# One transformer layer on one core: a group later for the softmax normalisation, four banks for the last tiles, one chain of statistics

## The chip, the cores and the metric

The kernel runs on one core of a Trainium2 chip. The metric is the device time of one execution in microseconds (us). The profiler's page and trace come from one further execution, whose own time is given beside them.

## The reference

What is computed, cut to its core (4 batches of 1024 tokens of 256 numbers, 16 heads of 64, 32 experts with 1024 hidden numbers, all in float32):

```python
xn = (x - mean(x)) / sqrt(var(x) + 1e-5)
# attention, causal, q and k turned by the rotary table
q, k, v = heads(xn @ Wq), heads(xn @ Wk), heads(xn @ Wv)
attn = softmax(causal(rope(q) @ rope(k).T * 64 ** -0.5)) @ v
# experts choose tokens: the 8 likeliest tokens of each expert, over the softmax along the tokens
probs = softmax(xn @ gate_w.T + gate_b, axis=tokens)
vals, idx = top_k(probs, 8)
merged = sum_k(vals * xn[idx])                       # one row per batch and expert
h = gelu([merged, 1] @ w1[e]);  o = [h, 1] @ w2[e]
moe = zeros_like(x).at[idx].add(vals * o)
out = x + attn @ Wo + bo + moe
```

## The kernel before, in words

A pair is two heads of one batch. There are 8 pairs to a batch (`PAIRS`) and 32 in all (`N`). The program of every engine is one loop over `STAGES`, the list of (P, g) with pair P and group g = 0..5, after two groups of pair -1 that stand in for a beginning, and with pair 32 as a tail that has no scores. Within a stage each engine issues its instructions in an order written out by hand. Groups later or earlier in the list are reached by an index, as in `STAGES[s - 3]`.

In one group TensorE (PE) makes the scores of two chunks of the current pair into the PSUM tiles pA and pB (L1388 to L1400), makes the scores of the next pair once more for their row maxima, into bank 0 of pC and into pA (L1412, L1419), makes one projection into pF (the "fill": L1465 for q and k, L1448 for v), may do one further piece of work (below), multiplies the exponentials with V into pO (L1490), and twice per pair sums the exponentials' partial sums into pC (L1499).

The other engines follow it. VectorE (DVE) takes the maxima (L1065), which PE awaits before it goes on to the further piece of work; it combines them (L1072), makes the shift t_D from them (L1079), and does the rotary steps (L1099, L1089). ScalarE (ACT) takes the exponentials into t_PT (L812), evicts the projections (t_raw, L834) and rounds them (t_HI, L844). GpSimd (POOL) adds up the exponentials (t_acc, L732, L735), does two rotary steps (L710, L713) and adds the bias to the input rows (t_xb, L745). SyncE (SP) issues most DMAs in one queue of instructions: the swap of neighbouring rows for the rotary step (t_swap, L623), loads and stores.

**Normalising.** A half pair n (64 of them) ends in this chain: PE sums (L1499), ACT evicts (L861), SP stores the row (s_s, L522) and loads it spread over partitions (t_comp, L527), DVE inverts it (`invert`, L1049), SP stores it (r_s, L532) and loads it broadcast into the place t_OT (L553), and DVE multiplies the attention's output into it (`normalise`, L1057). `invert` runs two stages after the half pair's sums, `normalise` three stages after, as the last DVE instruction of its stage. For batch 0 SP then stores the normalised rows (o0_s, L658), to be loaded back when the output tiles of this batch are made.

**The further pieces.** Pairs 5 to 13 have the experts' work, in 4-expert groups, as slots: layer 1 (PE L1514, L1519), a turn, and layer 2; DVE reads each slot's bank. Output tiles of 128 tokens are 16 or 24 matmuls with Wo and one matmul with the spread matrix t_wsp of the experts: those of batch 0 in pairs 14 and 15 (L1546, L1548, rows t_os loaded by SP L682), of batches 1 and 2 in pairs 16, 17 and 24, 25 (L1540), from t_oh (rounded by ACT, L879) and t_ol (the rest, DVE L1133). The last batch's tiles are made in two pieces: `part` over seven pairs (L1561, L1564) in pairs 31 and 32, kept by DVE (`keep`, L1157), and `last` for pair 31 (L1573) at the end, finished by DVE (`finish`, L1163). ACT L887 and DVE L1150 round for the parts, in two buffers. The banks of these tiles are bank 1 of pC and of pB in turn (`out_bank`).

**Statistics.** The layer norm of batches 1 to 3 is prepared in pairs 0 to 2: bn_stats (L1171) and a chain of seven small dependent DVE instructions per batch (L1176 to L1184), a root on ACT (L893), and six more small ones (L1191 and on, `moments`). Units (L1595, L1624) transpose the rows of x, and are spread over pairs 1 to 3.

## Time and profile before

| what | value |
|---|---|
| time, median of 3 runs | 1408.34 us (1407.0 to 1410.91) |
| the profiled execution's own time | 1406.38 us |
| its span | 1404.6 us, mean granted TensorE clock 0.986 |
| PE, busy | 1331.6 us, 95% of the span |
| POOL, busy | 970.3 us, 69% |
| DVE, busy | 878.1 us, 63% |
| ACT, busy | 635.2 us, 45% |
| DMA read and written | 130.71 MB and 22.54 MB |

"L1057" is line 1057 of the kernel. A busy share says how much of the span an engine worked; which of them sets the end is to be read from the waits. The granted clock is that of TensorE, as a share of its 2.4 GHz.

### The profile page before, as it was taken

What the parts mean: (1) busy time and instruction counts of PE and PEld (TensorE: products, weight loads), DVE (VectorE), ACT (ScalarE), POOL (GpSimd) and SP (SyncE); (2) the same over time, 40 slices, a digit from 0 to 9 for tenths busy, and PEclk for the clock granted to TensorE, in tenths of its full rate; (3) what the DMA queues carried; (4) which work ended last, traced back from release to release, by engine and by line L of the source; (5) the groups of instructions that cost most, each with busy time, mean ns of one, the idle gap of its engine ahead of it and who ended that gap; (6) DMA issues with size and microseconds to landing.
All of it is one profiled execution on the core that took longest, in us unless ns stands there. A gap on an engine that the chain in (4) does not pass through costs nothing.

```text
span 1404.6 us, 31395 instructions
## 1 busy us (share of the span) xinstructions
PE 1331.6 (95%) x11612; PEld 867.7 (62%) x11612; DVE 878.1 (63%) x1202; ACT 635.2 (45%) x963; POOL 970.3 (69%) x661
## 2 busy tenths in 40 slices
PE   6889999999999999999999999999999999999987
PEld 5556566555655555546676776666656776666655
DVE  5797767666565556556347666666666566666633
ACT  3446565453445334524224434444444344554431
POOL 2666688765566656656566777888778668888842
PEclk9999999999999999999999999999999999999999
DMA  5324333669667866665642222212232221212121
GB/s 177 122 84 145 114 134 116 226 211 320 213 230 244 287 215 221 212 235 171 180 137 81 66 75 65 77 62 77 96 102 91 74 76 55 84 62 77 47 58 57
DMA packets 122752, 188.86 MB, mean 134 GB/s; under 512 B 29616, under 2 KB 57808, under 8 KB 122608
## 3 DMA queue, kind: packets, MB, share of 16 engines
q1 hardware_dynamic: 92176, 112.51, 24.4%
q10 hardware_dynamic: 30384, 74.23, 15.4%
q8 instruction: 100, 1.64, 0.5%
q14 instruction: 44, 0.36, 0.1%
q0 software_dynamic: 48, 0.13, 0.1%
HBM read 130.71 MB, written 22.54 MB: 109 GB/s over the span
## 4 chain that ended last, share of the span: by engine, by line
PE 79%; DMA 7%; DVE 5%; issue 4%; ACT 4%; SPq 1%; POOL 0%; ACTq 0%; DVEq 0%; POOLq 0%
PE t_pO L1490 17%; PE t_pF L1465 11%; PE t_pA L1388 9%; PE t_pB L1388 6%; PE t_pF L1448 6%; DMA t_swap<-t_raw 3%; PE t_pA L1412 3%; PE t_pC L1412 3%; PE t_pA L1393 2%; PE t_pC L1499 2%; PE t_pB L1393 2%; PE t_pB L1540 2%; PE t_pC L1540 2%; PE t_pB L1514 1%; ACT t_PT L812 1%
## 5 line engine op out<-in xcount | busy, mean ns | idle before, releaser
L735 POOL TENSOR_TENSOR t_acc<-t_acc,t_PT 128x1024 f32<-128x1024 f32 (+3 forms) x256 | 437.9, 1711 | 161.8 <-ACT t_PT L812 141.6
L710 POOL TENSOR_TENSOR t_swap<-t_swap,t_sin 128x512 f32<-128x512 f32 x124 | 163.8, 1321 | 198.9 <-DMA t_swap<-t_raw 198.3
L1490 PE MATMUL t_pO<-t_PT,t_V 128*64 128x512 f32 (+3 forms) x1536 | 294.1, 504 | 4.7 <-issue 4.7
L812 ACT ACTIVATE t_PT<-t_pA 128x1024 f32<-128x1024 f32 x192 | 169.7, 884 | 273.1 <-PE t_pA L1400 234.7
L1465 PE MATMUL t_pF<-t_xT,t_wqk 128*128 128x512 f32 x756 | 211.2, 415 | 5.3 <-issue 3.0
L1490 PEld LDWEIGHTS t_pO<-t_PT,t_V 128*64 128x64 f32 x1536 | 94.3, 137 | 145.7 <-issue 129.3
L713 POOL TENSOR_TENSOR t_rot<-t_rot,t_swap 128x512 f32<-128x512 f32 x124 | 174.1, 1404 | 10.8 <-DVE t_rot L1099 1.2
L1465 PEld LDWEIGHTS t_pF<-t_xT,t_wqk 128*128 128x128 f32 x756 | 133.9, 190 | 41.3 <-issue 13.8
L834 ACT ACTIVATE t_raw<-t_pF 128x512 f32<-128x512 f32 x124 | 74.0, 597 | 180.5 <-PE t_pF L1465 136.6
L1089 DVE TENSOR_TENSOR t_LO<-t_rot,t_HI 128x512 fp32r<-128x512 f32 x124 | 147.1, 1186 | 7.5 <-ACT t_HI L844 7.5
L732 POOL TENSOR_TENSOR t_acc<-t_PT 128x768 f32<-128x768 f32 x64 | 142.9, 2232 | 9.6 <-ACT t_PT L812 9.6
L1065 DVE TENSOR_REDUCE t_nm<-t_pC 128x2 f32<-128x256 f32 (+2 forms) x96 | 71.8, 777 | 122.0 <-PE t_pC L1419 121.6
L812 ACT ACTIVATE t_PT<-t_pB 128x768 f32<-128x768 f32 (+1 forms) x192 | 141.9, 739 | 2.9 <-PE t_pB L1393 2.1
L1057 DVE TENSOR_TENSOR t_OT<-t_OT,t_OC 128x512 f32<-128x512 f32 x64 | 83.5, 1305 | 56.1 <-DMA t_OT<-r_s 56.1
L1065 DVE TENSOR_REDUCE t_nma<-t_pC 128x2 f32<-128x1024 f32 x66 | 80.7, 1222 | 54.2 <-PE t_pC L1412 54.1
L1448 PE MATMUL t_pF<-t_wvs,t_xT 128*128 128x256 f32 x756 | 106.6, 290 | 2.2 <-issue 2.1
L1448 PEld LDWEIGHTS t_pF<-t_wvs,t_xT 128*128 128x128 f32 x756 | 94.0, 190 | 11.8 <-issue 10.4
L1099 DVE TENSOR_TENSOR t_rot<-t_pF,t_cos 128x512 f32<-128x512 f32 x124 | 85.0, 685 | 22.4 <-ACT t_raw L834 19.1
L861 ACT ACTIVATE t_srow<-t_pC 128x256 f32<-128x256 f32 x64 | 24.6, 385 | 161.1 <-PE t_pC L1499 161.0
L1079 DVE TENSOR_TENSOR t_D<-t_pB,t_sel 128x512 fp32r<-128x512 f32 x64 | 43.9, 686 | 79.1 <-PE t_pB L1476 79.1
L1388 PE MATMUL t_pA<-t_HI 64*128 64x512 f32 (+1 forms) x384 | 88.9, 460 | 4.2 <-DVE t_nma L1065 2.7
L1388 PEld LDWEIGHTS t_pA<-t_HI 64*128 64x128 f32 x384 | 35.8, 183 | 85.1 <-issue 78.0
(228 smaller groups left out, 2465.3 us busy)
## 6 DMA issues: line engine op xcount, KB each, us to landing
t_w1t<-in_L_ffn_w ACTq DMA_DIRECT2D x32, 1024.0 KB, 5.5
t_w2t<-in_L_ffn_w ACTq DMA_DIRECT2D x32, 1024.0 KB, 8.4
t_swap<-t_raw SPq DMA_DIRECT2D x248, 128.0 KB, 2.1
t_OT<-r_s SPq DMA_DIRECT2D x128, 128.0 KB, 2.9
...
```

The source lines that it names most:

```text
L710: pool.tensor_tensor(swap_of(r), swap_of(r), sin[:, c * BANK:(c + 1) * BANK], ALU.mult).then_inc(sin_sem, 1)
L713: pool.tensor_tensor(rot_of(r), rot_of(r), swap_of(r), ALU.add).then_inc(rot_sem, 1)
L732: pool.tensor_tensor(a[:, :, off:], first[:, :, off:], pt, ALU.add).then_inc(acc_done, 1)
L735: pool.tensor_tensor(a[:, :, off:], a[:, :, off:], pt, ALU.add).then_inc(acc_done, 1)
L812: act.activation(PT[:, n % PTS, :, 0:w], bank[:, :, 0:w], ACT.Exp, scale=SCALE).then_inc(exp_done, 1)
L1065: op = dve.tensor_reduce(dst, bank[:, :, at:at + w], AX_X, ALU.max, negate=True)
L1089: dve.tensor_tensor(LO[:, P % 2, z, q], rot_of(r), HI[:, P % 2, z, q].bitcast(F32), ALU.subtract).then_inc(lo_done, 1)
L1099: dve.tensor_tensor(rot_of(r), fill_bank(f), cos[:, c * BANK:(c + 1) * BANK], ALU.mult).then_inc(cos_done, 1)
L1388: pe.matmul(bank[:, h, 0:w], hk[d, P % 2, 1, k], hq[d, P % 2, 0, q], start=(a == 0), stop=False)
L1448: mm = pe.matmul(bank[:, u * 2 * P128:(u + 1) * 2 * P128], xT[:, c, hx, k, q], wvs[:, hw, k, :], start=(a == 0), stop=(a == 3 * KT - 1))
L1465: mm = pe.matmul(bank, wqk[:, hw, k, z * P128:(z + 1) * P128], xT[:, c, hx, k, :], start=(a == 0), stop=(a == 3 * KT - 1))
L1490: mm = pe.matmul(pO[h * DH:(h + 1) * DH, off:], v, PT[:, n % PTS, h, 0:w], start=(j == 0), stop=(j == 4 * c + 3))
```

## The change

Four edits are made at once.

1. `normalise` on DVE moves from the end of the third stage after the sums into the middle of the fourth (after the maxima, the shift, the rotary steps and `invert`, ahead of the reads of slots and tiles). The last three of the 64 half pairs stay at the third stage. SP's store of the normalised rows of batch 0 goes one stage later too.
2. The output tiles of batch 0 are made one group later, (14,2) to (15,3) in place of (14,1) to (15,2), and their loads are issued one stage later; the first of them loses its special place behind the values.
3. The last batch's parts are rounded in three buffers instead of two, at stages of a list of their own (`ROUND_AT`); their banks are bank 1 of pC and pF, and they stand ahead of the wait for the second chunk's exponentials. Its last matmuls use four banks.
4. The statistics of batches 1 to 3 are one chain over all 24 tiles at (1,1), one root on ACT and one `moments` at (1,2), in place of three of each; batch 1's normalisation and its units move one group later.

The third buffer, oh3 and ol3, takes the place of xT, so a rounding into it waits until the last fill is done.

```diff
--- before.py
+++ after.py
@@ -113,7 +113,7 @@
 
     y, p = divmod(P, PAIRS)
     if MOE + E // GE <= P <= MOE + E // GE + 1:
-        n = (P - MOE - E // GE) * GROUPS + g - 1
+        n = (P - MOE - E // GE) * GROUPS + g - 2
         return [(0, n)] if 0 <= n < NT else []
     if P == N:
         tiles = {2: (0, 1, 2, 3), 3: (4, 5, 6, 7)}.get(g, ())
...
@@ -125,20 +125,22 @@
 PARTS_AT = {(N - 1, 1): [0], (N - 1, 2): [1], (N - 1, 3): [2], (N - 1, 4): [3], (N - 1, 5): [4], (N, 1): [5], (N, 2): [6, 7]}
 
 
+ROUND_AT = {(N - 1, 0): [0], (N - 1, 1): [1], (N - 1, 2): [2, 3], (N - 1, 3): [4], (N - 1, 4): [5], (N - 1, 5): [6], (N, 0): [7]}
+
+
 def parts_of(P, g):
 
     return PARTS_AT.get((P, g), [])
 
 
-UNITS_AT = {(0, 5): ("logit", 0), (1, 3): ("x", 1, 0), (1, 4): ("x", 1, 1), (2, 2): ("logit", 1), (2, 3): ("x", 2, 0),
+UNITS_AT = {(0, 5): ("logit", 0), (1, 4): ("x", 1, 0), (1, 5): ("x", 1, 1), (2, 2): ("logit", 1), (2, 3): ("x", 2, 0),
             (2, 4): ("x", 2, 1), (3, 2): ("logit", 2), (3, 3): ("x", 3, 0), (3, 4): ("x", 3, 1), (4, 2): ("logit", 3),
             (5, 0): ("gates",), (5, 1): ("merge",), (5, 2): ("merged",)}
 UNIT = {u: n for n, u in enumerate(UNITS_AT.values())}
 DOUBLE = {u: n for n, u in enumerate([u for u in UNIT if u[0] in ("x", "logit", "gates")])}
 UNIT_STEP = {u: UNIT[u] + sum(DOUBLE[v] < len(DOUBLE) and UNIT[v] < UNIT[u] for v in DOUBLE) for u in UNIT}
-STATISTICS_AT = {(0, 2): [(1, 0)], (0, 3): [(1, 1)], (0, 4): [(2, 0)], (0, 5): [(2, 1), (3, 0)], (1, 0): [(3, 1)]}
-MOMENTS_AT = {(1, 1): 1, (1, 4): 2, (2, 1): 3}
-NORM_AT = {(1, 2): (1, 0), (1, 3): (1, 1), (2, 2): (2, 0), (2, 3): (2, 1), (3, 2): (3, 0), (3, 3): (3, 1)}
+STATISTICS_AT = {(0, 2): [(1, 0)], (0, 3): [(1, 1)], (0, 4): [(2, 0)], (0, 5): [(2, 1)], (1, 0): [(3, 0)], (1, 1): [(3, 1)]}
+NORM_AT = {(1, 3): (1, 0), (1, 4): (1, 1), (2, 2): (2, 0), (2, 3): (2, 1), (3, 2): (3, 0), (3, 3): (3, 1)}
 NORM = {h: n for n, h in enumerate([(0, 0), (0, 1)] + list(NORM_AT.values()))}
 
 
...
@@ -257,7 +259,8 @@
         mT = sb("t_mT", [P128, GE, KT, 32])
         hT = sb("t_hT", [P128, 2, P128])
         with nc.sbuf_tensor("t_yp", [P128, NT, C], F32) as yp, nc.sbuf_tensor("t_wlast", [P128, C], F32) as wlast:
-            pass
+            with nc.sbuf_tensor("t_oh3", [P128, PAIRS - 1, P128], F32R) as oh3, nc.sbuf_tensor("t_ol3", [P128, PAIRS - 1, P128], F32R) as ol3:
+                pass
         xT = sb("t_xT", [P128, 2, 2, KT, BANK], F32R)
         wqk = sb("t_wqk", [P128, 2, KT, 2 * P128], F32R)
         wvs = sb("t_wvs", [P128, 2, KT, 2 * P128], F32R)
...
@@ -418,14 +421,28 @@
         y_stored = [sem(f"t_y_stored{i}") for i in range(2)]
         block = ctx.enter_context(nc.Block())
 
+        def rows_of(n):
+            return (slice(1, B), slice(0, NT)) if n == 2 else (0, slice(4 * n, 4 * n + 4))
+
         def next_outputs(s):
             return outputs_of(*STAGES[s + 1]) if s + 1 < len(STAGES) else []
 
-        def next_parts(s):
-            return parts_of(*STAGES[s + 1]) if s + 1 < len(STAGES) else []
+        def normalised_at(s):
+            late = normalise_of(*STAGES[s - 4]) if s >= 4 else None
+            soon = normalise_of(*STAGES[s - 3]) if s >= 3 else None
+            return [n for n in (late,) if n is not None and n < 2 * N - 3] + [n for n in (soon,) if n is not None and n >= 2 * N - 3]
 
         def parts_before(s):
             return sum(len(parts_of(*t)) for t in STAGES[:s])
+
+        def part_buffers(t):
+            return (oh3[:, :, :], ol3[:, :, :]) if t % 3 == 2 else (oh[:, t % 3, 0:PAIRS - 1, :], ol[:, t % 3, 0:PAIRS - 1, :])
+
+        def part_bank(t):
+            return (pC[:, 1, 0:C], pF[:, 0:C])[t % 2]
+
+        def last_bank(t):
+            return (pC[:, 1, 0:C], pF[:, 0:C], pB[:, 1, 0:C], pA[:, 1, 0:C])[t % 4]
 
         def fill_bank(f):
...
@@ -513,7 +530,7 @@
                             load_b2(G + 1)
 
             def tiles_ahead(P, g):
-                n = (P - MOE - E // GE) * GROUPS + g
+                n = (P - MOE - E // GE) * GROUPS + g - 1
                 return [0, 1] if n == -1 else [n + 2] if 0 <= n < NT - 2 else []
 
             def store_sums(n):
...
@@ -652,7 +669,7 @@
                     start_output(P // PAIRS)
                 if (P, g) == (N - 2, 5):
                     start_output(B - 1)
-                n = normalise_of(*STAGES[s - 4]) if s >= 4 else None
...
@@ -881,20 +898,22 @@
             def round_part(t):
 
                 act.wait_ge(o_done, 2 * (N - 2) + t // 4 + 1)
-                act.wait_ge(y_mm, (B - 1) * NT - 1 + min(t, 1))
-                if t >= 2:
-                    act.wait_ge(y_part, t - 1)
-                act.activation(oh[:, t % 2, 0:PAIRS - 1, :], OT[:, 0:PAIRS - 1, t * P128:(t + 1) * P128], ACT.Copy).then_inc(oh_done, 1)
+                act.wait_ge(y_mm, (B - 1) * NT)
+                if t == 2:
+                    act.wait_ge(proj_done, len(FILL))
+                if t >= 3:
+                    act.wait_ge(y_part, t - 2)
+                act.activation(part_buffers(t)[0], OT[:, 0:PAIRS - 1, t * P128:(t + 1) * P128], ACT.Copy).then_inc(oh_done, 1)
...
@@ -1023,9 +1042,8 @@
                     weights_high(w)
                 if (P, g) in UNITS_AT:
                     unit(UNITS_AT[P, g])
-                if (P, g) == (1, 1):
-                    for n in range(2, B + 1):
-                        root(n)
+                if (P, g) == (1, 2):
+                    root(2)
                 if (P, g) in NORM_AT:
...
@@ -1038,7 +1056,7 @@
                 for y, t in next_outputs(s):
                     if y in (1, 2):
                         round_out(y, t)
-                for t in next_parts(s):
+                for t in ROUND_AT.get((P, g), []):
                     round_part(t)
 
         @block.vector
...
@@ -1144,34 +1162,37 @@
             def rest_of_part(t):
 
                 dve.wait_ge(oh_done, (B - 2) * NT + t + 1)
-                dve.wait_ge(y_mm, (B - 1) * NT - 1 + min(t, 1))
-                if t >= 2:
-                    dve.wait_ge(y_part, t - 1)
-                dve.tensor_tensor(ol[:, t % 2, 0:PAIRS - 1, :], OT[:, 0:PAIRS - 1, t * P128:(t + 1) * P128],
-                                  oh[:, t % 2, 0:PAIRS - 1, :].bitcast(F32), ALU.subtract).then_inc(ol_done, 1)
+                dve.wait_ge(y_mm, (B - 1) * NT)
+                if t == 2:
+                    dve.wait_ge(proj_done, len(FILL))
+                if t >= 3:
+                    dve.wait_ge(y_part, t - 2)
+                high, low_part = part_buffers(t)
+                dve.tensor_tensor(low_part, OT[:, 0:PAIRS - 1, t * P128:(t + 1) * P128],
+                                  high.bitcast(F32), ALU.subtract).then_inc(ol_done, 1)
 
             def keep(t):
 
                 dve.wait_ge(y_part, t + 1)
                 dve.wait_ge(xb_done, (B - 1) * NT + t + 1)
-                dve.tensor_tensor(yp[:, t, :], out_bank(t), xb[:, t % 2, :], ALU.add).then_inc(y_kept, 1)
+                dve.tensor_tensor(yp[:, t, :], part_bank(t), xb[:, t % 2, :], ALU.add).then_inc(y_kept, 1)
 
             def finish(t):
 
                 dve.wait_ge(y_mm, (B - 1) * NT + t + 1)
                 dve.wait_ge(y_kept, NT)
-                dve.tensor_tensor(yp[:, t, :], out_bank(t), yp[:, t, :], ALU.add).then_inc(y_done, 1)
-
-            def statistics(n, h):
-
-                b = n - 1 if n > 1 else 0
-                c = slice(0, NT) if n > 1 else slice(4 * h, 4 * h + 4)
-                done = stat_done[n]
+                dve.tensor_tensor(yp[:, t, :], last_bank(t), yp[:, t, :], ALU.add).then_inc(y_done, 1)
+
+            def spread(b, h):
+
                 for t in range(4 * h, 4 * h + 4):
                     st = dve.bn_stats(stats[:, b, t, :], xn[:, b, t, :])
-                if n > 1 and h == 0:
-                    return
-                st.then_inc(done, 1)
+                return st
+
+            def statistics(n):
...
@@ -1322,8 +1345,7 @@
                 n = normalise_of(*STAGES[s - 2]) if s >= 2 else None
                 if n is not None:
                     invert(n)
-                n = normalise_of(*STAGES[s - 3]) if s >= 3 else None
-                if n is not None and P == N:
+                for n in normalised_at(s):
                     normalise(n)
                 w = weights_of(P, g)
...
@@ -1332,12 +1354,15 @@
                     unit(UNITS_AT[P, g])
                 for b, h in STATISTICS_AT.get((P, g), []):
                     dve.wait_ge(xb_loaded[b - 1], 32)
-                    statistics(b + 1, h)
+                    st = spread(b, h)
+                    if (b, h) == (B - 1, 1):
+                        st.then_inc(stat_done[2], 1)
+                        statistics(2)
                 if (P, g) == (0, 2):
                     dve.wait_ge(g_hi, 1)
                     dve.tensor_tensor(gThl[:, 1, :, :, :], gT[:, :, :, :], gThl[:, 0, :, :, :].bitcast(F32), ALU.subtract).then_inc(g_lo, 1)
-                if (P, g) in MOMENTS_AT:
-                    moments(MOMENTS_AT[P, g] + 1)
+                if (P, g) == (1, 2):
+                    moments(2)
...
                         rest(y, t)
-                for t in next_parts(s):
+                for t in ROUND_AT.get((P, g), []):
                     rest_of_part(t)
-                n = normalise_of(*STAGES[s - 3]) if s >= 3 else None
-                if n is not None and P < N:
-                    normalise(n)
 
...
@@ -1549,16 +1571,20 @@
 
             def part(t):
 
-                bank = out_bank(t)
+                bank = part_bank(t)
                 if t >= 2:
                     pe.wait_ge(y_kept, t - 1)
                 else:
                     pe.wait_ge(y_done, (B - 1) * NT)
+                    pe.wait_ge(max_done, MAXES[N, 0])
+                    pe.wait_ge(fill_read, len(VFILL))
+                    pe.wait_ge(cos_done, len(ROPE))
                 pe.wait_ge(ol_done, (B - 2) * NT + t + 1)
+                high, low_part = part_buffers(t)
                 a = 0
...
@@ -1566,11 +1592,12 @@
             def last(t):
 
                 pe.wait_ge(y_kept, NT)
-                if t >= 2:
-                    pe.wait_ge(y_done, (B - 1) * NT + t - 1)
+                pe.wait_ge(exp_done, N * len(CHUNKS))
+                if t >= 4:
+                    pe.wait_ge(y_done, (B - 1) * NT + t - 3)
                 pe.wait_ge(wo_loaded, 32)
                 pe.wait_ge(o_done, 2 * (N - 1) + t // 4 + 1)
-                pe.matmul(out_bank(t), OT[:, PAIRS - 1, t * P128:(t + 1) * P128], wlast[:, :],
+                pe.matmul(last_bank(t), OT[:, PAIRS - 1, t * P128:(t + 1) * P128], wlast[:, :],
                           start=True, stop=True).then_inc(y_mm, 1)
...
@@ -1690,6 +1716,8 @@
                     maximum(pair, MAXES[P, g] + m, (pC, pA)[m % 2], pieces)
                 if fill_of(P, g) and not after_gelu:
                     fill(fill_of(P, g))
+                for t in parts_of(P, g):
+                    part(t)
                 if chunks:
                     pe.wait_ge(exp_done, chunk_index(*chunks[1]) + 1)
                 if g == 1 and 0 <= P < N:
@@ -1703,20 +1731,16 @@
                 for x_ in slots:
                     if x_[0] == "turn":
                         slot(*x_)
-                for t in parts_of(P, g):
-                    part(t)
                 for y, t in outputs_of(P, g):
                     if y == B - 1:
                         last(t)
-                    elif not first_tile:
+                    else:
                         output(y, t)
                 for x_ in slots:
                     if x_[0] == "layer1":
                         slot(*x_)
                 for chunk in chunks:
                     values(*chunk)
-                if first_tile:
-                    output(0, 0)
                 for x_ in slots:
                     if x_[0] == "layer2":
                         slot(*x_)
```

## Rows read from the trace of the kernel before

**Rows 1.** The page's first part: busy time and share by engine.
```profile
PE 1331.6 (95%) x11612; PEld 867.7 (62%) x11612; DVE 878.1 (63%) x1202; ACT 635.2 (45%) x963; POOL 970.3 (69%) x661
```

**Rows 2.** Whom PE waited for: us in total, times, longest.
```profile
PE t_pB L1514 <- issue: 17.4, 8, 3.3
...
PE t_pO L1490 <- issue: 4.7, 3, 2.3
...
PE t_pC L1595 <- issue: 2.8, 1, 2.8
PE t_pA L1388 <- DVE t_nma L1065: 2.7, 1, 2.7
...
PE t_pB L1514 <- DVE t_nmb L1065: 1.7, 1, 1.7
...
PE t_pA L1393 <- DVE t_D L1079: 1.1, 1, 1.1
```

**Rows 3.** Timeline around one slot: start, us, engine line op, idle before.
```profile
387.30 0.69 DVE L1057 TENSOR_TENSOR t_OT<-t_OT,t_OC 128x512 f32<-128x512 f32 x1 [3.89 <-DMA t_OT<-r_s]
387.91 1.22 DVE L1065 TENSOR_REDUCE t_nma<-t_pC 128x2 f32<-128x1024 f32 x1
...
388.91 0.60 ACT L834 ACTIVATE t_raw<-t_pF 128x512 f32<-128x512 f32 x1 [2.27 <-DMA t_swap<-t_raw]
...
389.22 1.07 PE L1514 MATMUL t_pB<-t_w1t,t_mT 128*32 128x256 f32 x16 [1.83 <-issue]
```

**Rows 4.** Windows: length, busy PE, PEld, DVE, ACT, POOL, granted clock, DMA share, GB/s.
```profile
1350.00:1395.00 45.00, 37.52 (x297) 27.82 (x293) 11.97 (x19) 13.56 (x18) 19.00 (x14) 1.00 0.12 36
1395.00:1402.00 7.00, 4.44 (x17) 2.55 (x16) 4.42 (x10) 0.00 (x0) 0.00 (x0) 1.00 0.27 93
72.00:86.00 14.00, 11.28 (x93) 7.72 (x90) 13.03 (x23) 3.63 (x6) 10.70 (x7) 0.88 0.06 21
338.00:348.00 10.00, 7.10 (x61) 3.20 (x59) 7.93 (x11) 1.68 (x4) 4.99 (x4) 0.83 0.96 338
619.00:632.00 13.00, 9.66 (x68) 4.49 (x66) 4.92 (x7) 2.96 (x5) 8.99 (x7) 0.74 0.49 162
```

**Rows 5.** The chain of waits that ended last, stretch 380 to 392 us.
```profile
by line: DMA t_swap<-t_raw 99.2%; SPq L623 7.9%; SPq L553 5.1%; ACT t_raw L834 5.0%; SPq L658 4.9%; issue 2.5%; SPq L621 0.1%; ACTq L468 0.1%
```

**Rows 6.** Line L1057: idle time of DVE before it.
```profile
  DMA t_OT<-r_s: 56.1, 23
```

**Rows 7.** Timeline of batch 0's first two output tiles, PE and SP.
```profile
672.84 3.72 PE L1546 MATMUL t_pC<-t_wo,t_os 128*128 128x256 f32 x16
...
677.52 0.43 SPq L682 DMA_DIRECT2D t_os<-o_s  x1
...
678.44 0.70 PE L1548 MATMUL t_pC<-t_oe,t_wsp 128*128 128x256 f32 x2 [1.88 <-DMA t_oe<-o_s]
...
685.08 2.11 PE L1546 MATMUL t_pB<-t_wo,t_os 128*128 128x256 f32 x9
```

**Rows 8.** Line L682: the loads of batch 0's tiles.
```profile
DMA to landing us min/median/max: 4.3/4.9/5.5
```

**Rows 9.** Timeline where batch 1's first output tile begins.
```profile
772.97 2.33 DVE L1133 TENSOR_TENSOR t_ol<-t_OT,t_oh 128x1024 fp32r<-128x1024 f32 x1
...
775.69 0.48 PE L1540 MATMUL t_pC<-t_woh,t_oh 128*128 128x256 f32 x2
```

**Rows 10.** DVE timeline of the statistics chains: two of the three.
```profile
73.10 0.93 DVE L1176 TENSOR_TENSOR t_both<-t_stats 128x8 f32<-128x8 f32 x1
...
76.75 1.76 DVE L1184 SCALAR_TENSOR_TENSOR t_ve<-t_gap,t_mse 128x8 f32<-128x8 f32 x1
...
88.35 0.17 DVE L1176 TENSOR_TENSOR t_both<-t_stats 128x8 f32<-128x8 f32 x1
...
89.07 0.17 DVE L1184 SCALAR_TENSOR_TENSOR t_ve<-t_gap,t_mse 128x8 f32<-128x8 f32 x1
```

**Rows 11.** POOL timeline of the last pair.
```profile
1366.57 0.73 POOL L745 TENSOR_TENSOR t_xb<-t_xin,t_bob 128x256 f32<-128x256 f32 x1
```

24 lines of the change are left out of this document (14 added, 10 removed).

## The prediction

> **What bounds the kernel now.** I read the page's busy shares first. PE works for 1331.6 us, 95% of its span, and the next engine, POOL, for 69% [rows 1]. So time can only come out of PE: out of the 73.0 us in which it stands still (1404.6 less 1331.6), and out of stretches in which its clock was lowered. I then read whom PE waited for [rows 2], went to the timeline at each of the longer waits, to see which instruction was late [rows 3], and last to windows around them, for the granted clock [rows 4].
>
> The waits before L1514, the first matmul of a layer-1 slot, are the largest group: 17.4 us in 8 waits, put down to "issue", and 1.7 us in one more [rows 2]. The timeline shows what they are. DVE stood 3.9 us before `normalise`, until the broadcast load t_OT<-r_s had landed; it then worked 0.7 us, and only then came to the next stage's first maxima (387.91, 1.22 us). PE, which must see those maxima before it goes on to the slot, started it at 389.22, 0.1 us after they ended [rows 3]. So `normalise` as the last DVE instruction of a stage passes a DMA's lateness to PE. After the longest such gaps the clock is low: 0.83 of 2.4 GHz over the 10 us from 338, and 0.74 over the 13 us from 619 [rows 4]. Two more stretches of 10 us, from 572 and from 1038, are like the first, so there are three of these and one of the other.
>
> **a. `normalise` a group later: -26.8.** The multiplication comes after the maxima, the shift and the rotary steps of the stage behind, some 7 us (1404.6 us over 198 stages is 7.1) after its present place. The load that it waits for has then landed, since the longest wait seen is about 4 us. What goes is 17.4 + 1.7 before the slots, and before the values (L1490) the longest wait of 2.3 and 1.0 of the other 2.4 [rows 2], which begin the same way: 22.4. The clock comes back with it. The mean of 0.83 over 10 us loses 1.7 us if PE had work all the while, and 0.17 of its 7.10 busy us, 1.2, if it counts for those alone; 0.74 over 13 us loses 3.4 or 2.5 [rows 4]. Three of the first and one of the second are 8.5 or 6.1; I take 7.4, near the middle. Against this, in the same stretch ACT's eviction t_raw waited 2.27 us for the swap's DMA and began at 388.91 [rows 3], with only 0.3 us between it and PE's start. When DVE no longer delays PE, that DMA does a little later: PE's next fill needs the bank. I put this at 0.4 in each of 8 steps, 3. The sum is -22.4 - 7.4 + 3 = -26.8. The bounds are -10 (the swap takes most of it back) and -31 (nothing eroded, the clock wholly back). The price of the move itself is nothing in busy time: the same 64 instructions. They stand ahead of the slot reads now, so what is queued behind a late load is no longer the maxima but a slot's read; that is rival D.
>
> **b. Rounding where a batch ends: +3.2.** The first tiles of batches 1 and 2 need the pair before them normalised. Now the rest t_ol is worked out at 772.97 to 775.30 and PE uses it at 775.69 [rows 9]. With `normalise` about one rotary step, one shift and one low part later, ACT's rounding and the rest come some 2 us later, of which 0.4 is slack: 1.6, twice. Bounds 0 (it hides) and +4.
>
> **c. Batch 0's tiles: +3.0.** PE waited 1.88 us in the first tile for t_oe, until 678.44 [rows 7]; that goes. But the tile loads are now issued behind SP's instructions that start the output, at the place of the one at 677.52 [rows 7], and land 4.3 to 5.5 us later, median 4.9 [rows 8]: 682.4. Without the tile at 672.84 PE starts the next group then and comes to its tile after what it now does between 679.14 (678.44 + 0.70) and 685.08, 5.9 us, of which I take off 0.8 for the lowered clock seen there: 678.0. It waits 4.4, 2.5 more than now, and I add 0.5 for the clock after a longer gap. Bounds 0 (the group before hides it) and +6.
>
> The Trainium skill ("DMA: Bandwidth & Descriptors", section "Issuing engines are not separate DMA queues") says that DMAs of all issuing engines run on the same 16 DMA engines and interleave. By that rule the two tile loads issued together would share with each other and with the swap; if this doubled the 4.9 us of [rows 8], c would be +7.9 in place of +3.0. No row of before has two tile loads at once under load.
>
> **d. The early block: -3.9.** PE waited 2.7 us for the maxima t_nma and 1.1 for t_D, each behind a statistics chain on DVE, and 2.8 before a unit (L1595) behind the third `moments` [rows 2]; the clock was 0.88 over the 14 us from 72, which is 1.7 [rows 4]. Together 8.3, all gone with the chains. The one chain is no longer than one of the three in instructions, but lands at (1,1). Its price depends on POOL: from 73.10 to the end of 76.75 + 1.76 the seven took 5.4 us while POOL was adding up exponentials, from 88.35 to 89.24 0.9 us while it stood still [rows 10]. At (1,1) POOL is adding up. I take the middle, 3, as what reaches PE (2.9), and 1.5 for the clock: -8.3 + 4.4 = -3.9. Bounds -8 (0.9, hidden) and +2 (a chain of 5.4 in full, the waits for `moments` at (1,2) behind the root, and the lowered clock).
>
> The Trainium skill ("GPSIMD Engine Reference", section "1. Specifications") lists that GpSimd's SBUF interfaces are shared with VectorE, with contention for DVE instructions in a 2-port mode or with two SBUF inputs. This speaks against the merged chain at its new place; the 5.4 against 0.9 us of [rows 10] agree. By it the upper price would hold, 2.4 more than I take, and d would be -1.5.
>
> **e. The tail: -7.3.** Between 1350 and 1395 PE is busy for 37.52 of 45 us, so 7.5 us are idle: about half before parts that wait for exponentials, half before the two last parts, which wait for their rounding in two buffers; from 1395 to 1402 it is busy for 4.44 of 7 [rows 4]. Parts placed ahead of the wait for exponentials fill the first half, a third buffer takes the second. The four banks of the last tiles bring 0.7 of the 2.6 us in the last stretch. But t_xb comes from POOL behind two accumulations, as at 1366.57 [rows 11], and with it y_kept, for which part t+2 waits: +0.9. The sum is -7.5 - 0.7 + 0.9 = -7.3. Bounds -4 and -9.
>
> **Sum.** -26.8 + 3.2 + 3.0 - 3.9 - 7.3 = -31.8. From the profiled execution's own 1406.38 (span 1404.6 and 1.8 around it) this makes 1374.6. The median of the runs is 1408.34, 2.0 above the profiled one, so I forecast 1376.5.
>
> **Rivals.**
> B: The swap's DMA takes DVE's place. In the stretch of [rows 5] the chain that ends last is 99.2% the DMA t_swap<-t_raw, with ACT's t_raw behind it [rows 3]. For it: DMA share 0.96 in the window from 338 [rows 4]. Against it: the share is 0.49 in the window from 619, where the clock was lowest [rows 4], and the fill's bank is needed only a stage later. Half of a, 13.4, is then lost: 1390. Chance 0.15.
> C: The tail is set by POOL. Then parts wait for y_kept instead of exponentials, 3.7 of e go, and 0.8 more for bias sums: 1381. For it: two accumulations of the exponentials precede each bias sum, as at 1366.57 [rows 11]. Against it: the sum for part t is wanted only two parts later. Chance 0.09.
> D: The change doesn't do what it says: the load is late in the new place too, or DVE's reads of the slot banks behind it stop PE the same. Then a is 0: 1403.4, at the edge of no change. Against it: a whole group between. Chance 0.07.
> E, slower: `normalise` in the middle is where DVE has no slack, and all of DVE's 56.1 us of standing before it (23 waits) [rows 6] fall on PE, not 22.4 as now. Then a is not -26.8 but +33.7: 1376.5 + 60.5 = 1437. It decides once the waits in the new place cost PE 32 us more than I forecast. Against it: the load is given a group more. Chance 0.05.
>
> **How the numbers follow.** My forecast has 0.64; its own range is 1368 to 1386, from the bounds of a to e taken partly together. Range for 8 in 10: 1364, where a, d and e come near their lower ends, to 1394, which takes in B and C; D and E, and the far ends of a, lie outside. 0.3% is 4.2 us, about what a measurement here tells from no change, so faster means below 1404.1. Forecast, B and C are faster, and half of D: 0.91. The other half of D is the same: 0.04. E is slower: 0.05.
>
> **What would show it.** The profile after should have PE's waits before L1514 and its successor lines under 4 us in all, a granted clock near 1.0 in the windows where it was 0.83 and 0.74, and nearly no idle time of DVE before `normalise`. Right for c: a wait of PE in batch 0's first tile for t_os of about 4 us. Right for d: one chain of 3 us or more at (1,1), with a wait of PE in (1,2) behind it. Right for e: no wait for t_PT before the parts and none for t_ol. The forecast is wrong if PE's idle time stays above 50 us, or if new waits on ACT's t_raw, on t_swap or on y_kept stand where the old ones did.

## The result, and the profile after

The changed kernel takes 1393.24 us (median, 1389.95 to 1395.02) against 1409.21 us for the kernel before, measured beside it: ratio 0.9885, 95% interval 0.9861 to 0.9909, so 16 us faster. Measured once more, further below, it was 0.9871 (0.983 to 0.9911). The forecast was a fall of 31.8 us; it came to half.

The profiled execution took 1393.71 us, 12.7 less than the profiled one of before. The first parts of the page of the changed kernel:

```profile
span 1391.9 us, 31373 instructions
...
PE 1330.1 (96%) x11612; PEld 870.8 (63%) x11612; DVE 855.6 (61%) x1176; ACT 634.5 (46%) x961; POOL 975.7 (70%) x661
```

PE is as busy as before (1331.6 in [rows 1]), so nearly all of the gain is idle time: 61.8 us are left of 73.0. Whom PE waited for in the changed kernel (us in total, times, longest):

```profile
PE t_pF L1470 <- DMA t_wvs<-wv_s: 9.1, 3, 3.6
...
PE t_pC L1568 <- DMA t_os<-o_s: 4.9, 1, 4.9
PE t_pO L1512 <- issue: 4.4, 1, 4.4
...
PE t_pB L1410 <- ACT t_PT L829: 3.0, 3, 1.0
PE t_pF L1470 <- issue: 2.8, 4, 0.9
...
PE t_pB L1410 <- DVE t_g L1133: 2.3, 4, 1.0
```

The waits before the layer-1 slots, 17.4 and 1.7 us in [rows 2], are gone, and so are those before the values at 1038.67 and 1172.41. The one before the values now listed is in pair 1. New are 9.1 us in three waits for the load of t_wvs, 4.9 us for t_os, and eight of 0.3 to 1.0 us before L1410, the scores of a stage's second chunk. DVE has no idle time left before `normalise` (L1075 after; 56.1 us in [rows 6]).

Windows of the changed kernel (length, busy PE, PEld, DVE, ACT, POOL, clock, DMA share, GB/s):

```profile
340.00:350.00 10.00, 9.40 (x89) 5.38 (x87) 5.95 (x12) 5.33 (x9) 5.57 (x6) 1.00 1.06 367
350.00:360.00 10.00, 6.38 (x50) 5.22 (x48) 2.97 (x5) 6.64 (x9) 7.24 (x7) 0.76 0.64 239
535.00:550.00 15.00, 11.94 (x90) 7.60 (x90) 5.93 (x9) 6.43 (x11) 9.34 (x7) 0.77 0.30 110
1034.00:1044.00 10.00, 9.54 (x88) 5.75 (x87) 6.20 (x8) 6.14 (x11) 9.36 (x8) 1.00 0.41 134
1337.00:1382.00 45.00, 43.33 (x356) 32.55 (x357) 16.08 (x25) 16.42 (x23) 23.77 (x19) 1.00 0.16 41
1382.00:1389.00 7.00, 5.00 (x24) 3.51 (x22) 4.24 (x10) 0.00 (x0) 0.00 (x0) 1.00 0.31 103
```

The stretch near 1038 has its clock back (0.83 before), and so have those from 572 and from 619, where the granted clock is now 1.00. The one from 350 has not: 0.76, behind a wait of 3.6 us. In the tail PE is busy for 43.33 of 45 us (37.52 in [rows 4]).

To see where the 12.7 us went, I set the start of one and the same score matmul (L1388 before, L1410 after, counted from the first) in the two traces side by side. This is a table made from the two timelines:

```
before    after   after less before   stretch that ends here                       change
  58.31    62.17   +3.9               the start; no edit touches it                 +3.9
 260.16   266.01   +5.9               pairs 1 to 4                                  +2.0
 632.94   627.75   -5.2               pairs 5 to 13, the experts                   -11.0
 649.33   644.42   -4.9                                                             +0.3
 755.21   754.63   -0.6               batch 0's output tiles                        +4.3
1033.54  1033.50    0.0               first tiles of batch 1, pairs up to 23        +0.5
1048.59  1044.51   -4.1               the wait at 1038.67                           -4.0
1167.85  1164.18   -3.7               first tiles of batch 2                        +0.4
1179.40  1174.72   -4.7               the wait at 1172.41                           -1.0
1316.02  1311.33   -4.7               to pair 31                                     0.0
1404.6   1391.9   -12.7               the tail, to the end of the span              -8.0
```

The +3.9 of the start is in a part that no edit touches. In the traces of the further runs below the same mark lies between 58.5 and 64.3 us, so it is a difference between executions, and of the size of what separates -12.7 from -16.

### The profile page after: what moved, and what is told of

It reads as the page before. It is cut to its first block, busy times and chain, and to the rows that moved or that the text cites. A ratio compares the mean times of both kernels' runs of the same rounds, so it can differ in the third digit from the quotient of the medians.

```text
span 1391.9 us, 31373 instructions
## 1 busy us (share of the span) xinstructions
PE 1330.1 (96%) x11612; PEld 870.8 (63%) x11612; DVE 855.6 (61%) x1176; ACT 634.5 (46%) x961; POOL 975.7 (70%) x661
## 4 chain that ended last, share of the span: by engine, by line
PE 79%; DMA 8%; DVE 5%; issue 3%; ACT 2%; SPq 1%; POOL 1%; ACTq 0%; DVEq 0%; POOLq 0%
PE t_pO L1512 17%; PE t_pF L1487 11%; PE t_pA L1410 9%; PE t_pF L1470 7%; PE t_pB L1410 7%; DMA t_swap<-t_raw 4%; PE t_pA L1434 3%; PE t_pC L1434 3%; PE t_pA L1415 2%; PE t_pC L1521 2%; PE t_pB L1415 2%; PE t_pC L1562 2%; PE t_pB L1562 2%; DMA t_wvs<-wv_s 1%; PE t_pC L1568 1%
## 5 line engine op out<-in xcount | busy, mean ns | idle before, releaser
L727 POOL TENSOR_TENSOR t_swap<-t_swap,t_sin 128x512 f32<-128x512 f32 x124 | 167.8, 1353 | 183.7 <-DMA t_swap<-t_raw 183.2
L730 POOL TENSOR_TENSOR t_rot<-t_rot,t_swap 128x512 f32<-128x512 f32 x124 | 180.4, 1455 | 9.7
L1107 DVE TENSOR_TENSOR t_LO<-t_rot,t_HI 128x512 fp32r<-128x512 f32 x124 | 142.5, 1149 | 7.4 <-ACT t_HI L861 7.4
L749 POOL TENSOR_TENSOR t_acc<-t_PT 128x768 f32<-128x768 f32 x64 | 140.1, 2189 | 8.3 <-ACT t_PT L829 8.3
L1410 PE MATMUL t_pA<-t_HI 64*128 64x512 f32 (+1 forms) x384 | 89.1, 460 | 2.5 <-DVE t_nmb L1083 2.5
L1410 PEld LDWEIGHTS t_pA<-t_HI 64*128 64x128 f32 x384 | 35.8, 183 | 82.9 <-issue 78.3
L1083 DVE TENSOR_REDUCE t_nmb<-t_pC 128x2 f32<-128x256 f32 (+1 forms) x62 | 31.7, 554 | 87.3 <-PE t_pC L1441 87.3
L1434 PE MATMUL t_pC<-t_HI 64*128 64x512 f32 (+2 forms) x448 | 78.9, 372 | 4.2 <-ACT t_HI L861 2.1
```

The costliest lines, as they stand in the source:

```text
L727: pool.tensor_tensor(swap_of(r), swap_of(r), sin[:, c * BANK:(c + 1) * BANK], ALU.mult).then_inc(sin_sem, 1)
L730: pool.tensor_tensor(rot_of(r), rot_of(r), swap_of(r), ALU.add).then_inc(rot_sem, 1)
L749: pool.tensor_tensor(a[:, :, off:], first[:, :, off:], pt, ALU.add).then_inc(acc_done, 1)
L1083: op = dve.tensor_reduce(dst, bank[:, :, at:at + w], AX_X, ALU.max, negate=True)
L1107: dve.tensor_tensor(LO[:, P % 2, z, q], rot_of(r), HI[:, P % 2, z, q].bitcast(F32), ALU.subtract).then_inc(lo_done, 1)
L1410: pe.matmul(bank[:, h, 0:w], hk[d, P % 2, 1, k], hq[d, P % 2, 0, q], start=(a == 0), stop=False)
```

## The experiments

All ratios are against the kernel before, measured beside the kernels in question. There are three such groups (e1 to e4, e5 to e8, e9 to e11), each on a chip of its own; the kernel before had medians of 1413.46, 1413.66 and 1412.89 us in them, and its runs spread over 1400 to 1426 us. An interval is 4 to 8 us to each side.

**Edit 1 alone.** The kernel before with:

```diff
-                n = normalise_of(*STAGES[s - 3]) if s >= 3 else None
-                if n is not None and P == N:
+                for n in normalised_at(s):
                     normalise(n)
...
-                n = normalise_of(*STAGES[s - 3]) if s >= 3 else None
-                if n is not None and P < N:
-                    normalise(n)
```

and the store of batch 0 at `s - 5`.

> The kernel before with edit 1 alone (normalise in the middle of the fourth stage, the store of batch 0 one stage later). Theory X, a load that is late next: the waits before the layer-1 slots and before the values (22.4 us) go, but PE then waits for the load t_wvs<-wv_s, which SP issues behind the swap and the stores of a slot: about 9 us in three waits and 3 us of lowered clock, as in the changed kernel. Net of the pairs with experts -11, of the later pairs -5, and 3 to 5 us lost in pairs 1 to 5 where normalise now stands ahead of the reads of the units' banks: 10 to 14 us below the kernel before. Theory Y, my forecast as it stood: the t_wvs wait in the changed kernel comes from something else among its edits, and edit 1 alone gives -27. Theory Z: edit 1 gives nothing or little, and the changed kernel's gain comes from its tail.

Measured: 1405.15 us, ratio 0.9938 (0.9905 to 0.997), 8.8 us faster. Whom PE waited for:

```profile
PE t_pF L1449 <- DMA t_wvs<-wv_s: 9.9, 3, 3.4
...
PE t_pB L1389 <- ACT t_PT L817: 3.0, 3, 1.0
...
PE t_pB L1389 <- DVE t_g L1120: 2.3, 3, 1.5
```

The waits before the slots are gone and 9.9 us of waits for t_wvs have come, with edits 2, 3 and 4 absent. They belong to edit 1. My forecast as it stood (-27) falls; theory X's count of waits holds, its sum is a little too good (-10 to -14, against an interval of -4 to -13). It had put the loss in pairs 1 to 5 at 3 to 5 us; the trace has pairs 1 to 4 alone 7.4 us longer than the trace of before (the table at the end of this section).

**The load two groups earlier.** The changed kernel with:

```diff
-                unit = (P + 1) // 2
-                if g == 0 and P % 2 and PAIRS // 2 <= unit < N // 2:
+                unit = P // 2 + 1
+                if g == 4 and P >= 0 and P % 2 == 0 and PAIRS // 2 <= unit < N // 2:
```

> The changed kernel with one more edit: SP issues the load of t_wvs for pair P+1 at group 4 of pair P (P even), two groups ahead of its place before. Theory X, the load is only issued late: its three waits of 3.6, 3.1 and 2.4 us go and the clock of these stretches comes back, 10 to 12 us below the changed kernel, so some 26 to 28 below the kernel before. Theory V, the pairs with experts are held by the transfers of w1 and w2 whatever the order: the waits only move to another load (t_w1t, t_w2t, t_swap), and no more than 3 us go.

Measured: 1397.77 us, ratio 0.9872 (0.9813 to 0.9932), the same as the changed kernel (0.9871 and 0.9885). Waits and, under it, the timeline at one of them:

```profile
PE t_pB L1410 <- DVE t_g L1133: 10.0, 5, 2.8
```

```profile
348.58 0.60 ACT L851 ACTIVATE t_raw<-t_pF 128x512 f32<-128x512 f32 x1 [4.56 <-DMA t_swap<-t_raw]
...
349.21 0.69 DVE L1117 TENSOR_TENSOR t_rot<-t_pF,t_cos 128x512 f32<-128x512 f32 x1 [3.55 <-ACT t_raw L851]
...
349.82 0.68 DVE L1075 TENSOR_TENSOR t_OT<-t_OT,t_OC 128x512 f32<-128x512 f32 x1
...
350.42 0.42 DVE L1133 TENSOR_TENSOR t_g<-t_pB,t_b 128x256 f32<-128x256 f32 x1
...
350.89 0.33 PE L1410 MATMUL t_pB<-t_HI 64*128 64x128 f32 x2 [2.23 <-DVE t_g L1133]
```

The waits for t_wvs went, and 10.0 us in 5 waits stand before L1410 instead. The load itself, issued earlier, took 5.2 us at the median and up to 9.0, against 3.6 and 7.1 in the changed kernel. The timeline reads backwards: PE starts once DVE has read the slot's bank (350.42), which stood behind `normalise` (349.82) and the rotary step (349.21), which waited for ACT's t_raw (348.58), which had waited 4.56 us for the swap's DMA. Theory X, that the load was only issued late, falls. This is my rival B's chain, but it appears only once the other transfer is out of its way.

**Edit 4 undone.** The changed kernel with the three chains, roots and moments of the kernel before.

```diff
-                    if (b, h) == (B - 1, 1):
-                        st.then_inc(stat_done[2], 1)
-                        statistics(2)
+                    if h == 1:
+                        st.then_inc(stat_done[b + 1], 1)
+                        statistics(b + 1)
```

> The changed kernel with edit 4 undone: three statistics chains, roots and moments as in the kernel before. Theory S, the merged chain costs more than the three: the wait of 4.4 us before the values at 104.9 and its lowered clock (about 2) go, but the wait of 2.7 at 78 with its clock (4.5 together), the one of 1.1 at 101 and the one of 2.8 at 143 come back: within 3 us of the changed kernel. Theory F, as I forecast: edit 4 gained 3.9, so this kernel is 4 us slower than the changed one. If instead the loss of pairs 1 to 3 is all the merged chain's, it is 5 us faster.

Measured: 1399.31 us, ratio 0.9903 (0.9865 to 0.9942). Against 0.9871 that is 4.5 us slower, the size that theory F, my forecast, has; but the intervals overlap, and the ratio alone can't tell it from theory S.

**The reads first.** The changed kernel with `normalise`, up to pair 13, behind the reads of units and slots, in the same stage:

```diff
                 for n in normalised_at(s):
-                    normalise(n)
+                    if not behind(n):
+                        normalise(n)
...
+                for n in normalised_at(s):
+                    if behind(n):
+                        normalise(n)
                 for y, t in next_outputs(s):
```

> The changed kernel with normalise, up to pair 13, behind the reads of the units' and slots' banks instead of ahead of them, still in the fourth stage. Theory Q: the waits of PE before the second chunk's scores (L1410, 0.4 to 1.0 us, eight of them, near 128, 169, 210, 288, 347 and 531) are DVE's multiplication in front of the reads of bank pB; they go, 4 to 6 us below the changed kernel. Rival: the place inside the stage doesn't matter, or the maxima of the next stage come later by the 0.7 us of the multiplication instead, and the time is within 2 us of the changed kernel.

Measured: 1386.98 us, ratio 0.9797 (0.9751 to 0.9843). Against the changed kernel's 0.9871 that is 10 us less, more than the 4 to 6 expected. DVE's timeline at one of the places:

```profile
164.93 0.19 DVE L1070 RECIPROCAL t_rcomp<-t_comp 128x8 f32<-128x8 f32 x1
165.03 0.64 DVE L1233 TENSOR_TENSOR t_xs<-t_pC,t_xs 128x512 fp32r<-128x512 f32 x1
165.59 0.69 DVE L1233 TENSOR_TENSOR t_xs<-t_pB,t_xs 128x512 fp32r<-128x512 f32 x1
166.19 0.69 DVE L1078 TENSOR_TENSOR t_OT<-t_OT,t_OC 128x512 f32<-128x512 f32 x1
```

The unit's two banks are read directly behind `invert`, and the multiplication comes after. In the changed kernel it stood between `invert` and the two reads, and PE waited 0.99 us for bank pB, from 168.77:

```profile
166.91 1.29 DVE L1075 TENSOR_TENSOR t_OT<-t_OT,t_OC 128x512 f32<-128x512 f32 x1
168.12 0.68 DVE L1230 TENSOR_TENSOR t_xs<-t_pC,t_xs 128x512 fp32r<-128x512 f32 x1
168.72 0.67 DVE L1230 TENSOR_TENSOR t_xs<-t_pB,t_xs 128x512 fp32r<-128x512 f32 x1
```

```profile
169.76 0.33 PE L1410 MATMUL t_pB<-t_HI 64*128 64x128 f32 x2 [0.99 <-ACT t_PT L829]
```

The profile puts this wait down to ACT's exponentials of pA. But the kernel has PE wait here for DVE's read of pB (L1702), and in e4 PE began the same scores at 166.73, before those exponentials began (166.93). Of the waits of about 1.0 us before the second chunk's scores near 128, 169, 210 and 288, one of 0.6 is left (at 283). Theory Q holds. By the table at the end of this section the gain lies in pairs 1 to 4 (199.4 us in place of 204.2, e4 and e7 against the two traces of the changed kernel) and perhaps in pairs 5 to 13 (361 in place of 364, where two traces of the changed kernel differ by 4.8).

**A quarter of the weights.** The changed kernel, with the loads of w1 and w2 cut to a quarter from the third expert on:

```diff
-                act.dma_start(w1t[:, e % 2, :, :], w1[e, 0:C, :]...
+                n = HID if e < 2 else HID // 4
+                act.dma_start(w1t[:, e % 2, :, 0:n], w1[e, 0:C, 0:n]...
```

and so for w2. It works on stale weights for the rest; no matmul is left out.

> The changed kernel, but from the third expert on the loads of w1 and w2 fetch a quarter of each (256 of 1024 hidden units; the matmuls run on what is there, all of them). It leaves out three quarters of most weights. Theory V, the transfers of w1 and w2 fill the DMA engines and make the load of t_wvs and the swap late: the three waits before L1470 (9.1 us) and most other waits in pairs 6 to 13 go, the load of t_wvs lands in under 4 us, and the time is 10 to 14 us below the changed kernel. Theory X, SP's queue issues the load too late: the waits stay at 2 to 3 us each, at most 2 us less in all.

Measured: 1377.11 us, ratio 0.9743 (0.9698 to 0.9789), 18 us below the changed kernel by the ratios. Its windows:

```profile
340.00:350.00 10.00, 9.80 (x106) 5.20 (x103) 6.74 (x9) 4.21 (x7) 8.04 (x8) 1.00 0.46 156
350.00:360.00 10.00, 9.45 (x81) 6.73 (x83) 6.20 (x12) 8.78 (x12) 6.54 (x7) 1.00 0.43 145
535.00:550.00 15.00, 15.00 (x152) 8.70 (x149) 8.76 (x13) 5.22 (x8) 9.38 (x5) 1.00 0.27 79
```

and the landing times of the loads of t_wvs, first in the changed kernel and then in this one:

```profile
DMA to landing us min/median/max: 3.4/3.6/7.1
```

```profile
DMA to landing us min/median/max: 3.1/3.4/4.3
```

No wait before the fill from t_wvs over 0.6 us is left, the slowest load takes 4.3 us instead of 7.1, and PE has 9.80, 9.45 and 15.00 us of work in windows where it had 9.40, 6.38 and 11.94. The DMA share from 340 is 0.46, where it was 1.06. With a quarter of the bytes, and no order changed, the waits go: the transfers of w1 and w2 made the others late. This is shown, theory V. The time fell by more than the 10 to 14 us expected: the smaller loads also took away waits that the kernel before had already, as ACT's t_raw waited 44.0 us in all for the swap before, 34.2 in the changed kernel and 12.8 here. The kernel before with a quarter of the weights was not run, so what of the 18 us is the change's own loss is not shown by this run.

**Reads ahead of the rotary step.** The kernel of e4 with the early load of e2 and:

```diff
+                early = [x_ for x_ in slots_of(P, g) if x_[0] == "layer1"]
+                for x_ in early:
+                    read_slot(*x_)
                 if fill_of(P, g) in ROPE:
                     rope(fill_of(P, g))
```

> The kernel of e4_reads_first with two more edits: the load of t_wvs two groups earlier, as in e2_early_wv, and on DVE the reads of the layer-1 slots ahead of the rotary step, which waits for the swap through ACT's t_raw. Theory W: in e2 the waits before L1410 (2.2, 2.0, 2.8, 1.6 us) were DVE's read of the slot behind a rotary step that waited for t_raw, so behind the swap; with the reads first they go and the t_wvs waits stay away: 8 to 10 us below e4_reads_first. Theory V, the transfers are the bound in these pairs: the waits move on to the fill's bank (t_raw) or to t_w1t, and the time is within 3 us of e4_reads_first.

Measured: 1389.36 us, ratio 0.983 (0.9792 to 0.9868), 4.7 us slower than e4 (0.9797) by the ratios, with overlapping intervals. Waits:

```profile
PE t_pF L1480 <- issue: 8.2, 7, 2.0
...
PE t_pF L1497 <- issue: 6.0, 5, 2.4
```

They stand before the fills now, 8.2 us, and 6.0 of which 2.4 are at the start. The timeline at one:

```profile
342.94 0.60 ACT L854 ACTIVATE t_raw<-t_pF 128x512 f32<-128x512 f32 x1 [5.62 <-DMA t_swap<-t_raw]
...
343.57 0.69 DVE L1120 TENSOR_TENSOR t_rot<-t_pF,t_cos 128x512 f32<-128x512 f32 x1 [3.81 <-ACT t_raw L854]
...
344.37 2.90 PE L1497 MATMUL t_pF<-t_xT,t_wqk 128*128 128x512 f32 x6 [1.88 <-issue]
```

ACT's t_raw waited 5.62 us for the swap's DMA, DVE's rotary step waited for t_raw, and only after it is the bank pF free for PE's next fill. Theory W falls, and theory V's mechanism stands again: three orders, and each time a wait for a transfer is left, in another place.

**The tiles' loads in their old place.** The kernel of e4 with:

```diff
-                return [0, 1] if n == -1 else [n + 2] if 0 <= n < NT - 2 else []
+                return [0, 1] if n == -2 else [n + 2] if 0 <= n < NT - 2 else []
```

> The kernel of e4_reads_first with the loads of batch 0's first two tiles issued at (13,5) again, ahead of the instructions that start the output, and the tiles' matmuls one group later as in the change. The wait for t_os (4.1 to 5.2 us) goes and the lowered clock behind it (about 1.6): 5 to 6 us below e4_reads_first if the issue place is the cause. Rival: t_wsp and t_oe are now behind the two loads and PE waits as long for them: no change.

Measured: 1381.9 us, ratio 0.9778 (0.9746 to 0.9811). No wait for t_os is left; one of 1.3 us stands before the next scores at 671. By the ratios it is 2.7 us below e4, by the spans of the two profiled executions 6.4; the intervals overlap, so that the wait goes is shown, and the size not by the ratios. In the traces the stretch of batch 0's tiles takes 120.3 us here and 120.2 in e11, which has the same loads, against 125.0 in e4 and 125.7 in e6: some 5 us, as expected. This is the fastest full kernel of the study, and its interval lies below both of the changed kernel's.

**Edit 3 alone.** The kernel before with the last batch's parts of the change. For pair 31 the end-of-stage `normalise` moves into the middle of its stage.

```diff
-                for t in next_parts(s):
+                for t in ROUND_AT.get((P, g), []):
                     rest_of_part(t)
```

> The kernel before with edit 3 alone, the last batch's parts in three buffers and other banks; for pair 31 normalise moves from the end to the middle of its stage, which the new places of the rounding need. My ledger of the two traces gives the tail -8.0, the forecast gave -7.3: 6 to 9 us below the kernel before. Rival: part of the tail's gain came from edit 1, which had normalise a stage later there: then 3 to 5 us.

Measured: 1403.27 us, ratio 0.9926 (0.9896 to 0.9957), 10.5 us faster (6 to 15). Its tail, in windows 15 us later than the changed kernel's:

```profile
1352.00:1397.00 45.00, 44.33 (x361) 33.18 (x361) 15.10 (x25) 15.97 (x23) 23.18 (x18) 1.00 0.16 45
1397.00:1404.00 7.00, 3.96 (x16) 2.87 (x16) 4.30 (x10) 0.00 (x0) 0.00 (x0) 1.00 0.34 113
```

44.33 busy us of 45, against 37.52 in [rows 4]. The tail's gain needs none of the other edits: the rival, that part of it came from edit 1, falls.

**The changed kernel again, edit 4 alone, and edit 4 undone in the best kernel.** The three were measured together. Edit 4 alone is the kernel before with the statistics of the change; the last is e7 with the edit of e3.

> The changed kernel again, on the chip of the two kernels beside it. By its first result (0.9885 of the kernel before) some 16 us below the kernel before; the two better placed ones, measured in other calls against their own runs of before, were 0.9797 and 0.9778, so 12 and 15 us lower than this one should come out.

Measured: 1394.75 us, ratio 0.9871 (0.983 to 0.9911). Against it e4 is 10 us lower and e7 13, a little less than the 12 and 15 expected.

> The kernel before with edit 4 alone, one statistics chain. The forecast's term was -3.9 (bounds -8 and +2). The ledger of the two traces has -4.5 near 80, -3.0 near 140, and up to +5.6 between 101 and 133, part of which is edit 1's: between -3 and +2 us, so no difference that can be measured. Rival: the chain of 5.2 us under a busy POOL is the loss of pair 1, and this kernel is 5 us slower than the kernel before.

Measured: 1409.03 us, ratio 0.9968 (0.9934 to 1.0002), 4.5 us faster, with no change just inside the interval.

> The kernel of e7_tiles_loaded_early with edit 4 undone. If one chain and three are worth the same, this is within 3 us of e7 (0.9778 of the kernel before), and edit 4 can be left out. If the merged chain pays once nothing else is late in pair 1, it is 4 us slower than e7; if its long stretch on DVE costs, 4 us faster.

Measured: 1385.73 us, ratio 0.9818 (0.9779 to 0.9857), 5.7 us slower than e7 by the ratios. So edit 4 has three readings: -4.5 from e10, -4.5 from e3 and -5.7 from e11. Each alone is within its uncertainty of nothing, all have one sign.

**The stretches of all traces.** With the marks of the table above, the stretch up to 260.16 is pairs 1 to 4, up to 632.94 pairs 5 to 13, up to 755.21 batch 0's tiles, and from 1316.02 on the tail. This is a table made from the thirteen timelines, in us:

```
kernel                               pairs 1 to 4   5 to 13   batch 0's tiles   tail
before                                      201.8     372.8             122.3   88.6
e10, edit 4 alone                           202.1     377.3             124.5   89.4
e8, edit 3 alone                            203.7     377.8             122.1   79.4
e1, edit 1 alone                            209.3     363.9             120.7   91.5
e3, edit 4 undone                           210.5     367.5             125.2   80.5
changed kernel                              203.8     361.7             126.9   80.6
e9, the same                                204.5     366.5             124.2   80.6
e2, t_wvs loaded early                      204.3     365.0             126.4   80.6
e5, a quarter of the weights                206.0     346.5             125.5   80.6
e4, reads first                             199.3     361.2             125.0   80.5
e6, also t_wvs early, reads earlier         201.6     359.8             125.7   80.6
e7, e4 with tiles loaded early              199.5     360.8             120.3   82.0
e11, e7 with edit 4 undone                  205.0     363.8             120.2   80.6
```

Two traces of one kernel differ by up to 5 us in pairs 5 to 13, so single differences say little there, and groups say more. Edit 1 costs 6 to 9 us in pairs 1 to 4 while the statistics are three chains (e1 and e3 against before and e8), and 2 to 4 with one chain (e10 against the four with edit 1). So edit 4 is worth 5 to 7 us in this stretch where edit 1 is present (e3 and e11 against the changed kernel and e7), and nothing that can be seen where it is absent (e10). In pairs 5 to 13 the three kernels without edit 1 take 373 to 378 us, those with it 360 to 368, and e5 346.5.

## Why the forecast was half right

The direction was right, and so was the reading of which waits would go. What takes their place was not. The forecast fall of 31.8 us was 15.8 more than that of the medians and 19.1 more than that of the profiled executions. By the prediction's own sign it was wrong: PE's idle time is 61.8 us, above the 50 that it named.

**a, -26.8: the step that failed.** Its gross part held. The waits that I had picked from [rows 2], 22.4 us, all went, and no `normalise` waits for its load. What failed is the sentence that put the loss at 0.4 us in each of 8 steps, 3 in all. In the first table pairs 5 to 13 give -11.0, where waits of 19.1 us had stood and clock beside them, and -5.0 come later: -16.0 and not -26.8. With what edit 1 costs in pairs 1 to 4 it is less: e1, edit 1 alone, measured -8.8 (-4 to -13). Two things took the rest.

First, in the experts' pairs there are bursts in which the DMA engines have no time left, which [rows 4] had shown (DMA share 0.96 from 338), and I used the row only for a rival. Over the whole of these pairs the share is 0.70 before and 0.72 after. The chain of waits of the changed kernel from 340 to 357:

```profile
by line: DMA t_wvs<-wv_s 40.2%; DMA t_swap<-t_raw 37.2%; SPq L640 10.2%; SPq L528 8.2%; issue 3.9%; ACT t_raw L851 3.6%; PE t_pF L1470 3.2%; SPq L499 2.5%; ACTq L485 0.1%; SPq L661 0.1%
...
338.78 6.33 DMA t_swap<-t_raw
...
349.73 6.83 DMA t_wvs<-wv_s
```

A swap of 6.3 us and a load of 6.8. The load of t_wvs is late, 9.1 us in three waits, with the clock lowered behind them. The difference between the trace's -11.0 and a gross gain of some 25 (19.1 and most of the 7.4 of clock) is 14. e5 shows that the weights' bytes cause the late loads, and e2 and e6 that no order of issue tried here cures them. That they account for all of the 14 is not shown: e4 may have gained some 3 us in these pairs by the place of the multiplication. I had named a late transfer as what comes next, but took one in particular, the swap's, and asked what it would do in each step instead of asking how much idle time the DMA engines had to give. Rival B had the right kind of cause and the wrong transfer: ACT's waits for the swap did not grow, they fell from 44.0 to 34.2 us. That its 1390 is 3 us from the median is in part luck, for its price was half of a and came from no row.

The Trainium skill ("DMA: Bandwidth & Descriptors", section "Issuing engines are not separate DMA queues") says that DMAs started by different engines run on the same 16 engines and interleave. The runs agree: ACT issues w1 and w2, SP issues t_wvs, and the slowest load of t_wvs took 7.1 us beside whole weights and 4.3 beside a quarter of them.

Second, I put the price of the new place at "nothing in busy time", and had no other price for it in the sum. The busy time of the 64 multiplications indeed did not grow (83.5 us before, 78.0 after). But standing ahead of the reads, the multiplication keeps PE from bank pB for about 1 us at three units, near 128, 169 and 210, and for 0.3 to 1.0 us at some slots. I had said what is queued behind it, and had made of it only rival D. e4 shows the price: 10 us by the ratios, of which some 5 are in the waits that went. What the table can place of it lies in pairs 1 to 4, for which a had no term at all.

**b, +3.2.** It came to about +0.9 (0.5 and 0.4 in the table). I had counted each delay of the rounding in full; most of it lay under other work.

**c, +3.0.** +4.3 by the table. The mechanism was as forecast, and the wait for t_os was 4.9 us where I had 4.4:

```profile
672.21 1.00 SPq L699 DMA_DIRECT2D t_os<-o_s  x2
...
678.22 2.05 PE L1568 MATMUL t_pC<-t_wo,t_os 128*128 128x256 f32 x4 [4.89 <-DMA t_os<-o_s]
```

The two loads are issued at 672.21 and PE starts the tile 6.0 us later; the one load of [rows 8] took 4.9 at the median. That is above it but far from the doubling which the sentence on the skill worked out. All eight loads now land in 4.0 to 7.1 us, median 5.2. e7 then took the whole term away again by issuing the two loads one stage earlier.

**d, -3.9.** The trace gives +2.0 for pairs 1 to 4, of which three waits of 1.0 before the scores are edit 1's. The runs give -4.5, -4.5 and -5.7 (e3, e10, e11), and the traces 5 to 7 us less in pairs 1 to 4 where edit 1 is present, none where it is absent. So the number came out near -3.9, but I had added a and d as if neither changed the other, and they do. In detail the chain was dearer in the changed kernel than I took it:

```profile
103.15 1.21 DVE L1197 TENSOR_TENSOR t_both<-t_stats 128x24 f32<-128x24 f32 x1
...
105.77 2.31 DVE L1203 TENSOR_SCALAR t_mse<-t_square 128x24 f32<-128x24 f32 x1
108.12 0.18 DVE L1205 SCALAR_TENSOR_TENSOR t_ve<-t_gap,t_mse 128x24 f32<-128x24 f32 x1
```

Seven instructions from 103.15 to 108.30 are 5.2 us, near the upper price of 5.4 and not the middle. PE waited 4.4 us behind it (2.9 forecast). What the chain takes goes with GpSimd. In e4 it fell into a gap of GpSimd's work and took 1.0 us, from 102.83 to 103.87:

```profile
102.83 0.21 DVE L1200 TENSOR_TENSOR t_both<-t_stats 128x24 f32<-128x24 f32 x1
...
103.69 0.18 DVE L1208 SCALAR_TENSOR_TENSOR t_ve<-t_gap,t_mse 128x24 f32<-128x24 f32 x1
```

```profile
103.99 1.27 POOL L730 TENSOR_TENSOR t_swap<-t_swap,t_sin 128x512 f32<-128x512 f32 x1 [1.28 <-DMA t_swap<-t_raw]
```

So it is in all traces: the 8 chains of batches 1 to 3 that ran while GpSimd stood still (0.1 us of its work at most) took 0.9 to 1.05 us, with 8 or 24 columns alike, and the 15 beside its work 3.0 to 5.4. The middle that I took, 3, is a mean of two cases.

The Trainium skill ("GPSIMD Engine Reference", section "1. Specifications") lists SBUF interfaces shared by GpSimd and VectorE. The row agrees with the price that I had worked out by it, 5.4 us, better than with the middle that I took; that it is this sharing that stretches the chain was not tried apart; that the chain is long only beside GpSimd's work is seen in all 23 chains.

**e, -7.3.** -8.0 by the table, -10.5 (6 to 15) by e8. Right in kind and size. Rival C fell: no wait of a part for POOL's bias sums is in the list of PE's waits.

**Rivals D and E** fell by their times: in the new place DVE never waited for its load. But D's second half, that DVE's reads of the banks stop PE all the same, came true in small, and is the second thing above.

Term by term, against the profiled execution, a missed by 10.8 us, pairs 1 to 4 (d, with edit 1's cost there) by 5.9, c by 1.3, and the start, which no edit touches, added 3.9; b and e came out 2.3 and 0.7 better than forecast.
